# A wait in GpSimd's stream of gathers, moved behind the first gather of the next group

## The chip, the core and the metric

The kernel runs on one core of a Trainium2 chip. The metric is the device time of one execution in microseconds (us). The engines named here are TensorE (PE in the rows; its weight loads are PEld), VectorE (DVE), ScalarE (ACT), GpSimd (POOL) and SyncE (SP), which only issues transfers.

## The reference

For each of 512 samples, 26 embedding rows of 128 floats are looked up in 26 tables (1000 to 125000 rows each). The dense features are put in front as feature 0. The pairwise dot products of the 27 vectors are taken, and a three layer perceptron runs on the dense features and those products.

```python
e = jnp.stack([tbl_0[ids[:, 0]], ..., tbl_25[ids[:, 25]]], axis=1)      # 512 x 26 x 128
combined = jnp.concatenate([dense[:, None, :], e], axis=1)              # 512 x 27 x 128
interactions = jnp.einsum('bfd,bgd->bfg', combined, combined)
z = jnp.concatenate([dense, interactions[:, iu, ju]], axis=1)           # upper triangle, 351 pairs
h = jnp.concatenate([z, dense], axis=1)                                 # 512 x 607
h = jnp.maximum(h @ W_top1 + b_top1, 0.0)                               # 512
h = jnp.maximum(h @ W_top2 + b_top2, 0.0)                               # 256
y = h @ W_top3
```

## The kernel before

The 512 samples are four tiles of 128, t = 0 to 3. The rows of an embedding reach on-chip memory in one of two ways. Five features of every tile (six in the last two tiles) come from tables of 1000 rows that are loaded whole and multiplied by one-hot matrices on TensorE; the code calls such a step "hot". All other features are **gathered**: GpSimd issues one indirect transfer for each feature and tile, which fetches 128 rows of 512 bytes. Tiles 0 and 1 gather 21 features each, tiles 2 and 3 gather 20 each, 82 in all (line 419).

The gathers are put together in six groups for each tile, `g0` to `g5`, in the table `GROUPS`. Group 0 holds the dense features and three gathers, groups 1 to 4 hold four gathers (group 3 of tiles 2 and 3 holds three), group 5 holds two. Every group of every tile has a semaphore of its own, `rows_in[t][g]`, to which each of its gathers adds 16 when it has landed. TensorE waits on it ahead of the transposes of that group (line 681), and VectorE waits on groups 1 and 2 of tiles 2 and 3 ahead of dot products that it forms itself.

GpSimd walks through tiles, groups and gathers in that order. Ahead of a group's first gather it waits until all rows of the group before have landed (lines 414 to 417). From tile 2 on it also waits on `group_ps` ahead of the first gather of a tile, until TensorE has transposed the rows that stood in the same buffer two tiles earlier (`rows` has two slots, t % 2).

The order of the work on TensorE, ScalarE and VectorE is written out by hand in the table `ORDER`, one line for each tile. Its words are:

- `h`: eight chunks of one-hot products for one feature (lines 664, 667), stored by ScalarE at line 464
- `g0` to `g5`: the transposes of a group of the next tile (line 681), stored by ScalarE at line 485 or by VectorE at line 573. Products and transposes take turns in two banks of the product memory, so a step needs that the step two places before it is stored
- `u0`, `u1`: the pairwise products ("gram") of one half of this tile (line 702). ScalarE copies them to `z` (line 494), from tile 1 on together with VectorE (lines 586, 587)
- `x`, `l0` to `l3`, `e`, `y`: the perceptron (lines 647, 740, 752, 760 and 762), with its outputs taken out by ScalarE and VectorE
- `d`, `p`: dot products on VectorE and their transposition

So `u0` of a tile needs all six groups of that tile transposed and stored. For tiles 0 and 1 SyncE also moves parts of `z` by transfers once the copies are done, and the first layer waits for those.

```python
"h h g0 h g1 h g2 h g3-5",                       # ahead of tile 0
"u0 h u1 g0 h g1 h g2 h g3 h g4-5",              # tile 0, with the groups of tile 1 between
"u0-1 g0 h x0 l0:0 l1:0 g1 l2:0 l3:0 g2 e0 g3 d0-2:2 y0 x1 l0:1 l1:1 g4 d3-5:2 l2:1 g5 l3:1 e1",
"u0-1 y1 p2 d0-5:3 g0 x2 l0:2 g1 l1:2 g2 l2:2 g3 l3:2 e2 g4 y2 g5",
"u0-1 p3 x3 l0-3:3 e3 y3",
```

Of the kernel before, what the change touches and what calls it, by code (L numbers as in the profile page):

```python
# [27 lines left out]
def features(group):  # L28
    return [f + k for f, n in group for k in range(n)]
# [46 lines left out]
def dlrm_tower(nc, dense, ids, tables, w1, b1, w2, b2, w3, out):  # L76
# [20 lines left out]
    NG = len(GROUPS[0])  # L97
# [6 lines left out]
    gathered = [f for g in GROUPS[0] for f in features(g) if f]  # L104
# [43 lines left out]
    def fold_to(i):  # L148

        for k0, k1, src, _, to, at in folds():  # L150
            if k0 <= i // 4 < k1 and src // 32 == i % 4:
                return to + i // 4 - k0, at + 32 * (i % 4) + i + 1 - src


    assert all(m <= 4 * (to + k - k0) + at // 32 + 1 for k0, k1, _, m, to, at in folds() for k in range(k0, k1))
    PACKS = len(list(folds())) + 1

# [12 lines left out]
    def dot_at(i):  # L170

        first, _, _, at = PARTS[i >= PARTS[1][0]]
        return at + sum(NDOT - k for k in range(first, i))
# [26 lines left out]
    def groups_of(t):  # L200
        return GROUPS[t // HT]
# [4 lines left out]
    with ExitStack() as ctx:  # L206
        def sb(name, shape, dt=F32):
            return ctx.enter_context(nc.sbuf_tensor(name, shape, dt))

        def sem(name):  # L210
            return ctx.enter_context(nc.semaphore(name))

        ids_i = sb("ids_i", [P, T, NF - 1], I32)
# [3 lines left out]
        rows = sb("rows", [P, 2, len(gathered), D])  # L217
# [41 lines left out]
        rows_in = [[sem(f"rows_in{t}_{g}") for g in range(NG)] for t in range(T)]  # L259
# [140 lines left out]
        @block.gpsimd  # L400
        def _(pool):
            nc.gpsimd.memset(ident[:], 0.0).then_inc(ident_zeroed, 1)
            nc.gpsimd.iota(row_i[:], pattern=[[1, R8]], base=0, channel_multiplier=R8).then_inc(row_i_ready, 1)
            pool.wait_ge(ident_zeroed, 1)
            nc.gpsimd.affine_select(out=ident[:], in_=ident[:], compare_op=ALU.not_equal, fill=1.0, base=0,
                                    pattern=[[-1, P]], channel_multiplier=1).then_inc(ident_ready, 1)
            pool.wait_ge(ids_in, 16)
            for t in range(T):
                if t >= 2:

                    pool.wait_ge(group_ps, (t - 1) * NG)
                for g, group in enumerate(groups_of(t)):
                    if g:
                        pool.wait_ge(rows_in[t][g - 1], 16 * sum(f > 0 for f in features(groups_of(t)[g - 1])))
                    elif t:
                        pool.wait_ge(rows_in[t - 1][NG - 1], 16 * len(features(groups_of(t - 1)[NG - 1])))
                    for f in features(group):
                        if f:
                            pool.indirect_dma_start(  # L419
                                out=rows[:, t % 2, gathered.index(f), :], out_offset=None, in_=tables[f - 1],  # L420
                                in_offset=bass.IndirectOffsetOnAxis(ids_i[:, t, f - 1:f], 0),
                            ).then_inc(rows_in[t][g], 16)

        @block.scalar
        def _(act):
# [358 lines left out]
```

## Time and profile before

| what | value |
|---|---|
| median of 3 runs | 176.2 us (175.25 to 177.08) |
| the profiled execution's own time | 175.72 us |
| its span in the trace | 173.9 us |
| TensorE matmul busy | 118.4 us (68%) |
| TensorE weight load busy | 105.9 us (61%) |
| GpSimd busy | 79.8 us (46%), of it 79.0 us in 82 gathers |
| VectorE busy | 74.9 us (43%) |
| ScalarE busy | 72.3 us (42%) |
| mean granted TensorE clock | 0.80 of full speed |

The span runs from the first to the last recorded instruction; the execution's own time is 1.8 us longer. Busy shares are averages over stages with different limits. "issue" in a row is idle time of an engine for which the trace names no event. A gather's busy time is the time that GpSimd works on its descriptors; the rows land later.

### The profile page before, as it was taken

The numbers are of one execution on the slowest core, as the hardware profiler recorded it, in microseconds if no ns is written. First come the engines' busy times: TensorE is split into PE (matmuls) and PEld (weight loads), VectorE is DVE, ScalarE is ACT, GpSimd is POOL, SyncE is SP. The second block draws the span as 40 slices with busy tenths as digits, with TensorE's granted clock in tenths as the row PEclk, the third lists the DMA queues.
The fourth block names the chain that finished last, engine by engine and source line by source line (L and its number), as shares of the span: only waits on it lengthen the run. The fifth ranks groups of instructions, "written<-read, shape, count | busy, mean of one in ns | idle before, by whom it ended". The sixth has DMA issues, their size and how long they took to land.

```text
span 173.9 us, 2764 instructions
## 1 busy us (share of the span) xinstructions
PE 118.4 (68%) x1052; PEld 105.9 (61%) x1052; DVE 74.9 (43%) x181; ACT 72.3 (42%) x179; POOL 79.8 (46%) x89
## 2 busy tenths in 40 slices
PE   0699693621289729952886983849846499578694
PEld 0388583511189719841775983849735499467694
DVE  3699962960002545760062319900023994008200
ACT  7787873110109894421062831112023724208411
POOL 2662642644547547554645754546457455400000
PEclk9999879555557995795589999696987659969889
DMA  5645982573111111211111111211111112100000
GB/s 178 174 149 148 268 242 77 163 267 79 31 49 34 45 45 35 53 46 30 30 36 45 47 38 39 56 30 30 34 45 45 30 38 57 32 2 4 0 0 0
DMA packets 6290, 11.96 MB, mean 69 GB/s; under 512 B 2682, under 2 KB 3294, under 8 KB 6149
## 3 DMA queue, kind: packets, MB, share of 16 engines
q0 software_dynamic: 2624, 5.38, 12.1%
q1 hardware_dynamic: 3509, 6.15, 11.5%
q10 hardware_dynamic: 144, 0.26, 0.6%
q8 instruction: 8, 0.13, 0.3%
q14 instruction: 5, 0.04, 0.1%
HBM read 10.65 MB, written 0.00 MB: 61 GB/s over the span
## 4 chain that ended last, share of the span: by engine, by line
DMA 39%; POOL 32%; issue 15%; PE 8%; DVE 3%; POOLq 1%; ACT 0%
DMA rows<-in_tbl_dram,ids_i 37%; POOL rows L419 32%; PE ps L740 4%; DVE z L586 2%; PE ps L702 2%; DMA ids_i<-in_ids_dram 2%; PE ps L752 1%; PE ps L681 1%; POOLq L206 1%; PE ps L647 0%; DVE z L587 0%; PE ps L762 0%; ACT emb_t L485 0%; ACT y L521 0%; DVE h_t L614 0%
## 5 line engine op out<-in xcount | busy, mean ns | idle before, releaser
L419 POOL DMA_INDIRECT rows<-in_tbl_dram,ids_i x82 | 79.0, 964 | 70.1 <-DMA rows<-in_tbl_dram,ids_i 44.9
L552 DVE TENSOR_SCALAR hot<-ps,row_no 125x256 fp32r<-125x256 f32 x73 | 29.9, 474 | 26.0 <-PE ps L634 24.3
L681 PE MATMUL ps<-ident,rows 128*128 128x128 f32 x82 | 17.0, 333 | 30.8 <-DMA rows<-in_tbl_dram,ids_i 27.3
L494 ACT COPY z<-ps 32x80 f32<-32x80 f32 (+2 forms) x80 | 25.7, 321 | 28.3 <-remote 14.2
L681 PEld LDWEIGHTS ps<-ident,rows 128*128 128x128 f32 x82 | 11.0, 167 | 34.4 <-DMA rows<-in_tbl_dram,ids_i 30.0
L664 PE MATMUL ps<-hot,tab_hi 125*128 125x256 f32 x88 | 29.7, 357 | 2.8 <-ACT emb_t L464 1.5
L667 PE MATMUL ps<-hot,tab_lo 125*128 125x256 f32 x88 | 28.6, 345 | 1.2 <-DVE tab_lo L540 0.9
L702 PE MATMUL ps<-emb_t 128*64 128x52 f32 x512 | 23.9, 262 | 6.5 <-issue 3.7
L702 PEld LDWEIGHTS ps<-emb_t 128*64 128x64 f32 x512 | 22.0, 178 | 9.0 <-issue 6.3
L586 DVE COPY z<-ps 32x80 f32<-32x80 f32 (+2 forms) x42 | 13.1, 312 | 31.6 <-PE ps L702 18.6
L485 ACT COPY emb_t<-ps 128x512 f32<-128x512 f32 (+2 forms) x22 | 12.8, 580 | 32.5 <-PE ps L681 31.8
L664 PEld LDWEIGHTS ps<-hot,tab_hi 125*128 125x128 f32 x88 | 22.2, 253 | 3.9 <-ACT emb_t L464 1.7
L667 PEld LDWEIGHTS ps<-hot,tab_lo 125*128 125x128 f32 x88 | 22.1, 251 | 2.2 <-DVE tab_lo L540 1.2
L740 PE MATMUL ps<-z,w_pair 128*128 128x128 f32 x80 | 13.5, 334 | 2.1 <-DVE z L587 2.1
L740 PEld LDWEIGHTS ps<-z,w_pair 128*128 128x128 f32 x80 | 13.2, 250 | 2.6 <-ACT z L494 2.5
L614 DVE TENSOR_SCALAR h_t<-ps,b 128x128 f32<-128x128 f32 x4 | 1.4, 351 | 28.5 <-PE ps L752 28.5
L647 PE MATMUL ps<-emb_t,w_x 128*128 128x128 f32 x32 | 9.3, 403 | 4.4 <-issue 4.0
L509 ACT ACTIVATE h_t<-ps 128x128 f32<-128x128 f32 x16 | 4.4, 280 | 18.4 <-PE ps L740 12.1
L464 ACT COPY emb_t<-ps 128x256 f32<-128x256 f32 x11 | 6.6, 597 | 11.6 <-PE ps L667 8.7
L740 PEld LDWEIGHTS ps<-z,w_fold 128*128 128x128 f32 x64 | 9.8, 228 | 0.1
L740 PE MATMUL ps<-z,w_fold 128*128 128x128 f32 x64 | 9.7, 309 | 0.0
L752 PE MATMUL ps<-h_t,w 128*128 128x128 f32 x64 | 9.6, 311 | 0.0
(48 smaller groups left out, 96.4 us busy)
## 6 DMA issues: line engine op xcount, KB each, us to landing
tab<-in_tbl_dram SPq DMA_DIRECT2D x6, 448.0 KB
rows<-in_tbl_dram,ids_i POOLq DMA_INDIRECT x82, 2.6
w_fold<-w_pair SPq DMA_DIRECT2D x1, 1024.0 KB
w<-in_W_top_dram SPq DMA_DIRECT2D x1, 512.0 KB
tab<-in_tbl_dram SPq DMA_DIRECT2D x6, 52.0 KB
x_rows<-in_r_dense_features_dram ACTq DMA_DIRECT2D x1, 256.0 KB, 2.9
w_x<-in_W_top_dram SPq DMA_DIRECT2D x1, 256.0 KB
h_t<-in_W_top_dram SPq DMA_DIRECT2D x1, 256.0 KB
```

The source lines that it names most:

```text
L419: pool.indirect_dma_start(out=rows[:, t % 2, gathered.index(f), :], out_offset=None, in_=tables[f - 1], in_offset=bass.IndirectOffsetOnAxi ...
L485: nc.scalar.copy(*copies[-1]).then_inc(stored_act, 1)
L494: last = nc.scalar.copy(dst, src)
L552: nc.vector.tensor_scalar(hot[0:RP, k % OHB], ps[0:RP, IDV[h] + n % 2, 0:HB], row_no[0:RP, c:c + 1], None, ALU.is_equal).then_inc(hot_dve, 1)
L586: nc.vector.tensor_copy(dst, src)
L647: nc.tensor.matmul(block_ps(c), w_x[:, c * P:(c + 1) * P], emb_t[:, t, :, 0], start=True, stop=False)
L664: nc.tensor.matmul(bank, tab_hi[0:RP, n, c], one_hot, start=c == 0, stop=False)
L667: nc.tensor.matmul(bank, tab_lo[0:RP, n, c], one_hot, start=False, stop=c == R8 - 1).then_inc(hot_used, 1)
L681: last = nc.tensor.transpose(ps[:, ROT + bank_of(s), m * P:(m + 1) * P], src, ident[:])
L702: last = nc.tensor.matmul(ps[32 * q:32 * (q + GT), bank, col:col + GC], emb_t[:, t, b0:b0 + GT, :].rearrange("p b f -> p (b f)"), emb_t[:, ...
L740: last = nc.tensor.matmul(block_ps(c), weights[:, k, cols], z[:, t % 2, k, :], start=False, stop=k == nk - 1)
L752: last = nc.tensor.matmul(h2_ps(m), w_2[:, c, m * P:(m + 1) * P], h1_t[:, t % 2, c], start=c == 0, stop=c == NB - 1)
```

## The change

The wait for the group before is moved by one place: it stands behind the first gather of the new group and ahead of its second. The number of gathers, their order, their semaphores and all other engines' programs stay the same. The wait on `group_ps` at the start of tiles 2 and 3 stays ahead of the first gather.

```diff
                 for g, group in enumerate(groups_of(t)):
-                    if g:
-                        pool.wait_ge(rows_in[t][g - 1], 16 * sum(f > 0 for f in features(groups_of(t)[g - 1])))
-                    elif t:
-                        pool.wait_ge(rows_in[t - 1][NG - 1], 16 * len(features(groups_of(t - 1)[NG - 1])))
-                    for f in features(group):
-                        if f:
-                            pool.indirect_dma_start(
-                                out=rows[:, t % 2, gathered.index(f), :], out_offset=None, in_=tables[f - 1],
-                                in_offset=bass.IndirectOffsetOnAxis(ids_i[:, t, f - 1:f], 0),
-                            ).then_inc(rows_in[t][g], 16)
+                    fetched = [f for f in features(group) if f]
+                    for n, f in enumerate(fetched):
+                        if n == 1 and g:
+                            pool.wait_ge(rows_in[t][g - 1], 16 * sum(a > 0 for a in features(groups_of(t)[g - 1])))
+                        elif n == 1 and t:
+                            pool.wait_ge(rows_in[t - 1][NG - 1], 16 * len(features(groups_of(t - 1)[NG - 1])))
+                        pool.indirect_dma_start(
+                            out=rows[:, t % 2, gathered.index(f), :], out_offset=None, in_=tables[f - 1],
+                            in_offset=bass.IndirectOffsetOnAxis(ids_i[:, t, f - 1:f], 0),
+                        ).then_inc(rows_in[t][g], 16)
```

On GpSimd, at the start of tile 0 (the name behind `in_` is the table of a gather; `rows_in0_0` is group 0 of tile 0), the rows of both kernels differ like this:

```order
 L419 DMA rows<-in_tbl_1_dram,ids_i 128x128
 L419 DMA rows<-in_tbl_2_dram,ids_i 128x128
-L419 DMA rows<-in_tbl_18_dram,ids_i 128x128 [waits rows_in0_0]
-L419 DMA rows<-in_tbl_19_dram,ids_i 128x128
+L419 DMA rows<-in_tbl_18_dram,ids_i 128x128
+L419 DMA rows<-in_tbl_19_dram,ids_i 128x128 [waits rows_in0_0]
 L419 DMA rows<-in_tbl_20_dram,ids_i 128x128
 L419 DMA rows<-in_tbl_21_dram,ids_i 128x128
```

The gather from table 18, the first of group 1, no longer waits for group 0; the one behind it does. The same holds at every other border between two groups, 23 in all.

On GpSimd, around the start of tile 2, where a second semaphore is waited for:

```order
-L419 DMA rows<-in_tbl_7_dram,ids_i 128x128 [waits rows_in1_4]
-L419 DMA rows<-in_tbl_8_dram,ids_i 128x128
-L419 DMA rows<-in_tbl_0_dram,ids_i 128x128 [waits rows_in1_5,group_ps]
-L419 DMA rows<-in_tbl_1_dram,ids_i 128x128
+L419 DMA rows<-in_tbl_7_dram,ids_i 128x128
+L419 DMA rows<-in_tbl_8_dram,ids_i 128x128 [waits rows_in1_4]
+L419 DMA rows<-in_tbl_0_dram,ids_i 128x128 [waits group_ps]
+L419 DMA rows<-in_tbl_1_dram,ids_i 128x128 [waits rows_in1_5]
 L419 DMA rows<-in_tbl_2_dram,ids_i 128x128
```

The two waits that stood in front of one gather now stand in front of two different ones. In group 5, which has two gathers, the wait stands ahead of the last.

## Rows read from the trace of the kernel before

**Rows 1.** The chain of work that ended last, by engine, shares of the span.
```profile
DMA 39%; POOL 32%; issue 15%; PE 8%; DVE 3%; POOLq 1%; ACT 0%
```

**Rows 2.** Timeline, GpSimd, a quiet stretch: start, us, engine, line, [idle before <-releaser].
```profile
123.42 0.94 POOL L419 DMA_INDIRECT rows<-in_tbl_dram,ids_i  x1 [1.84 <-DMA rows<-in_tbl_dram,ids_i]
124.67 0.94 POOL L419 DMA_INDIRECT rows<-in_tbl_dram,ids_i  x1 [0.30 <-issue]
125.92 0.94 POOL L419 DMA_INDIRECT rows<-in_tbl_dram,ids_i  x1 [0.30 <-issue]
127.17 0.94 POOL L419 DMA_INDIRECT rows<-in_tbl_dram,ids_i  x1 [0.30 <-issue]
129.91 0.94 POOL L419 DMA_INDIRECT rows<-in_tbl_dram,ids_i  x1 [1.80 <-DMA rows<-in_tbl_dram,ids_i]
```

**Rows 3.** Waits of GpSimd, whole span: us in total, times, longest us.
```profile
POOL rows L419 <- DMA rows<-in_tbl_dram,ids_i: 44.9, 21, 5.4
```

**Rows 4.** Chain in order of time: from the last gather's start to its landing.
```profile
23.09 6.08 DMA rows<-in_tbl_dram,ids_i
...
33.18 3.10 DMA rows<-in_tbl_dram,ids_i
...
149.59 2.72 DMA rows<-in_tbl_dram,ids_i
```

**Rows 5.** Timeline, GpSimd, first gather of tile 2.
```profile
83.18 0.94 POOL L419 DMA_INDIRECT rows<-in_tbl_dram,ids_i  x1 [2.41 <-PE ps L681]
```

**Rows 6.** Timeline, TensorE: group transposes (L681) and gram (L702) of four tiles.
```profile
42.91 1.11 PE L681 MATMUL ps<-ident,rows 128*128 128x128 f32 x4 [5.47 <-DMA rows<-in_tbl_dram,ids_i]
...
48.63 3.66 PE L702 MATMUL ps<-emb_t 128*64 128x52 f32 x64 [1.04 <-ACT emb_t L485]
...
82.46 0.69 PE L681 MATMUL ps<-ident,rows 128*128 128x128 f32 x2 [2.98 <-DMA rows<-in_tbl_dram,ids_i]
83.91 6.31 PE L702 MATMUL ps<-emb_t 128*64 128x52 f32 x128 [0.77 <-ACT emb_t L485]
...
106.61 0.55 PE L681 MATMUL ps<-ident,rows 128*128 128x128 f32 x3 [2.87 <-DMA rows<-in_tbl_dram,ids_i]
...
113.38 0.65 PE L681 MATMUL ps<-ident,rows 128*128 128x128 f32 x4 [0.88 <-DMA rows<-in_tbl_dram,ids_i]
...
117.44 0.44 PE L681 MATMUL ps<-ident,rows 128*128 128x128 f32 x2 [2.07 <-DMA rows<-in_tbl_dram,ids_i]
...
122.54 2.58 PE L702 MATMUL ps<-emb_t 128*64 128x52 f32 x73
...
152.35 0.44 PE L681 MATMUL ps<-ident,rows 128*128 128x128 f32 x2 [2.27 <-DMA rows<-in_tbl_dram,ids_i]
153.66 5.27 PE L702 MATMUL ps<-emb_t 128*64 128x52 f32 x128 [0.88 <-ACT emb_t L485]
```

**Rows 7.** Waits of TensorE from 60 us to the end.
```profile
PE ps L681 <- DMA rows<-in_tbl_dram,ids_i: 13.2, 6, 3.0
```

**Rows 8.** Timeline, ScalarE: stores (L464, L485) and gram copies (L494).
```profile
77.76 0.59 ACT L464 COPY emb_t<-ps 128x256 f32<-128x256 f32 x1 [2.93 <-remote]
79.51 0.59 ACT L485 COPY emb_t<-ps 128x512 f32<-128x512 f32 x1 [1.16 <-PE ps L681]
...
87.91 2.81 ACT L494 COPY z<-ps 32x112 f32<-32x112 f32 x8 [4.36 <-PE ps L702]
...
129.24 2.42 ACT L494 COPY z<-ps 32x80 f32<-32x80 f32 x8 [7.92 <-remote]
```

**Rows 9.** Windows: stretch, length, busy us and (count) of PE, PEld, DVE, ACT, POOL, clock.
```profile
78.10:88.40 10.30, 6.26 (x87) 5.39 (x87) 0.47 (x2) 1.69 (x5) 4.72 (x5) 0.50 0.13 32
...
108.80:112.20 3.40, 3.40 (x18) 3.39 (x16) 3.16 (x8) 0.28 (x1) 2.36 (x3) 0.51 0.18 46
...
119.10:122.50 3.40, 3.40 (x17) 3.22 (x16) 0.00 (x0) 0.65 (x2) 1.89 (x2) 0.50 0.22 54
```

**Rows 10.** DMA queue of instructions: packets, MB, share of 16 engines.
```profile
q8 instruction: 8, 0.13, 0.3%
```

## Prediction

> **What bounds the kernel now.** I read the chain of work that ended last first. Transfers, GpSimd and its issue gaps fill 86% of it, TensorE 8% [rows 1]. The kernel is one long stream of gathers, with 20 us of other work behind the last. GpSimd's timeline shows the pattern. Four gathers start 1.25 us apart (0.94 busy and 0.30 to issue); then GpSimd sits idle 1.80 us, until the fourth has landed, and the next group's first gather starts 2.74 us behind it [rows 2]. There are 21 such waits, 44.9 us in total [rows 3], and two more at the starts of tiles 2 and 3, which the trace books to TensorE [rows 5]. The third view is TensorE's: what it waits for ahead of each tile's gram decides how much of a faster stream reaches the end. It stands idle 5.47 us ahead of one group of tile 0 and a few us more in later tiles [rows 6].
>
> **What one border costs, before and after.** Take the last gather of a group at time 0. Before, the next group's first gather starts at 2.74 and its second 1.25 later, at 3.99 [rows 2]. Now the first starts at 1.25 and is done at 2.19, while the landing that is waited for comes at about 2.5 in any case. The second then starts where the first stood, at 2.74. So each border gives 1.25 us, as long as the gather in flight doesn't hold up the landing. With 23 borders the stream of gathers gets 28.7 us shorter. At the starts of tiles 2 and 3 the two waits on one gather cost 2.41 us of idle time against 1.80 to 1.84 elsewhere [rows 2, 5]; split over two gathers, that 0.6 goes too, most likely (0.5 each taken, bounds 0 and 0.6). The last landing moves from 149.59 + 2.72 = 152.3 [rows 4] to about 152.3 - 28.7 - 1.0 = 122.6 us. TensorE can't follow that far, so the sum has to be made tile by tile at TensorE, at the start of each gram.
>
> **Tile 0.** The gram of tile 0 starts at 48.63, right behind the last two groups, for which TensorE waited [rows 6]. Five borders lie ahead of it: 5 x 1.25 = 6.2 us. TensorE's own work ahead of these groups ends long before (the idle 5.47 us of group 4 alone is nearly that). For the first three of these borders the row above doesn't hold, since table and weight loads are still moving and a landing takes 6.08 and 3.10 us there [rows 4]. If the gather that goes out early only queues in a line that is full already, those borders give nothing, and the gain is 2.5 us. If the idle line between groups is what is filled, they give more than 1.25 each, since each first gather then waits its long landing beside the previous one; I cap this at 8.7 us in all (2.5 us more). I take 6.2, as the borders with short landings give it and the idle line between groups is there in both cases.
> The trace shows that gathers land late only where the loads run [rows 4]. The Trainium skill, DMA: Bandwidth & Descriptors, section "Queues, rings and completion order", says that a DMA engine takes turns between the queues that have work for it, one packet at a time. By that, gathers beside loads go at the pace of their share, an earlier gather only waits earlier, and the three borders give near to nothing; the sum below would come to 160.1. The rows that are there before the change can't tell the two apart.
>
> **Tile 1.** Between tile 0's gram and the store at 77.76 [rows 8] no gather is waited for, so this piece moves as a whole. Then TensorE waited for groups 4 and 5, and the gram started at 83.91 [rows 6]. Without these waits, group 4 is transposed at once and its store (0.59) follows the one that ends at 78.35; group 5 needs the bank that this store frees, 0.69 for its two transposes, some 0.4 for its store and 0.4 to start: about 79.9. That gives 4.0 us (bounds 3.0, if the stores line up worse, and 5.1, the two idle times together). The rows are there: group 5's landing was at about 82.4 and ten to eleven borders have taken 12.5 to 13.7 us off it, against the 6.2 by which TensorE has moved.
>
> **Tile 2.** TensorE waited 2.87, 0.88 and 2.07 us for groups 3, 4 and 5 [rows 6], 5.8 us. Each landing is 18 us and more earlier by then, with TensorE 10 us earlier. What is late next is the first layer's wait for the moved parts of `z`, and stores on ScalarE, both nearly due at the same time. I take 5.5 (bounds 4.0 and 5.8).
>
> **Tile 3.** The last group's wait of 2.27 us [rows 6] goes. ScalarE's store of the group before and its copy of an output stand right behind it: 2.1 (bounds 1.5 and 2.3). The six waits of the last three tiles are 13.2 us by the view of waits [rows 7]; 11.6 of them count. From 153.66 on nothing of the tail (20.2 us) touches a gather, so it stays.
>
> **TensorE's clock.** The gram of tile 1, after idle time, ran with half the clock granted (1.2 in place of 2.4 GHz): its first half took from 83.91 to 87.91, 4.0 us [rows 6, 8, 9]. Two more stretches at half clock follow gather waits; in the three TensorE was busy 6.26 + 3.40 + 3.40 = 13.1 us [rows 9]. With the waits gone some of them may be granted in full, which halves their busy time: between nothing and 6.5 us. I take 2.0, the half of the one piece, those 4.0 us, on which both copying engines wait. The clock may as well fall at other places, which the rows of before can't show; I let that cost up to 1.5.
>
> **What stays.** VectorE and ScalarE started to copy the gram of tile 2 at 129.24 [rows 8], 6.7 us after it had begun at 122.54 with 73 matmuls in 2.58 us [rows 6]. There TensorE has gaps for which the trace names no event. I count them as unchanged. The page lists 8 instruction transfers of 0.13 MB together [rows 10]. The Trainium skill, Runtime: NRT & Kernel Launch, section "Instruction fetch mechanics", says that each engine's program is streamed in blocks of 16 KiB while it runs, at a cost that is mostly hidden. By that rule such gaps wouldn't be there; the trace doesn't agree if these gaps are fetches, which no row proves.
>
> **The sum.** 173.9 - 6.2 - 4.0 - 5.5 - 2.1 - 2.0 = 154.1 us of span. The execution's own time was 1.8 above its span, and the median of the runs 0.5 above that execution: 156.4 us.
>
> **Rivals.**
> - *Early borders give nothing and the clock stays.* For it: landings of 6.08 us [rows 4]. 156.4 + 3.7 + 2.0 = 162.1. Chance 0.17.
> - *More comes free.* The clock is granted in full at more places, tile 0 gains up to 8.7, or the gaps of tile 2 (6.7 us less the 2.58, 4.1) close as work shifts. For it: the low clock follows the waits for gathers [rows 6, 9]. About 156.4 - 2.5 - 2.5 = 151.4. Chance 0.18.
> - *The landing moves with the extra gather.* If a group counts as landed only when what is behind it in the queue is through, each landing comes later by what the border had given. Against it: within a group the gathers already follow at 1.25 us with the same number in flight, and the fourth lands 2.5 us after its start. At no gain per border the time is 176.2; at half of it tile 0 gains 3.1 and the later waits mostly still go, about 160 to 168. Chance 0.08.
> - *Slower.* The place is the same landing, with the point of decision at 1.25 us: if an extra gather in flight puts the landing back by more than that, every border loses. Were it by 1.5 us, 23 x 0.25 = 5.8 us would be lost on the path, 182 us. It could be so if GpSimd's descriptor work on the new gather held up the completion of the old one. Against it: that work is 0.94 us and over 0.3 us before the landing is due. Chance 0.02.
> - *The change doesn't do what it says.* GpSimd's order shows each wait moved by one gather at all borders; only if GpSimd stopped for the index list or a hidden limit of gathers in flight would the time stay at 176. Chance 0.02.
>
> **How the numbers follow.** The forecast as written, 153 to 160, has 0.53. With the rivals on either side, 151 to 164 holds about 8 in 10: it reaches 151.4 and 162.1 and a part of the third rival. A change of 1% (1.8 us) is about what a measurement of this kernel can tell from none. Faster by over 1%: 0.94, within 1%: 0.03, slower: 0.03.
>
> **What would show it.** In the profile after, GpSimd's idle time ahead of a group's second gather is about 0.55 us (2.74 - 1.25 - 0.94), its last gather starts near 120 us, and the chain of waits no longer runs through gathers behind tile 0. TensorE waits for rows in tile 0 alone, its grams start near 42.4, 73.7, 105 to 107 and 133 to 136 us, and the tail of 20 us is as long as before. I am wrong if the landing after a group's last gather is well over 2.6 us in the quiet part, if the gram of tile 0 starts later than 44, or if new idle time on ScalarE's or SyncE's side takes over in tile 2.

## The result and the profile after

The changed kernel took 147.63 us (147.18 to 148.24, four runs) against 175.85 us (175.25 to 177.08, four runs) for the kernel before: a ratio of 0.839, 95% interval 0.8333 to 0.8447. The forecast was 156.4 us with a range of 151 to 164, so the sign was right and the gain, 28.2 us, was larger than the range allowed. The experiments below add a second finding that matters more for anyone who wants to use the change: measured again on three other chips, the same changed kernel took 208 to 210 us, while the kernel before took 176 everywhere. First the execution that the forecast was about.

The page: the first row of busy times, and the chain of work that ended last.

```profile
PE 103.3 (71%) x1052; PEld 93.8 (65%) x1052; DVE 75.0 (52%) x181; ACT 72.3 (50%) x179; POOL 80.0 (55%) x89
...
DMA 46%; POOL 27%; issue 13%; PE 9%; DVE 3%; ACT 1%; POOLq 0%
```

Against [rows 1], nothing has taken the place of the gathers: transfers, GpSimd and issue gaps are still 86% of the chain, and the span is 145.4 us in place of 173.9. The waits of GpSimd and of TensorE, whole span (us in total, times, longest):

```profile
POOL rows L419 <- DMA rows<-in_tbl_dram,ids_i: 21.0, 22, 3.6
...
PE ps L681 <- DMA rows<-in_tbl_dram,ids_i: 17.7, 9, 4.2
```

GpSimd's waits fell from 44.9 us [rows 3] to 21.0. TensorE, though, still waits nine times for gathers, seven of them behind 60 us, which the forecast had said it would not do behind tile 0. GpSimd's timeline after, a quiet stretch and the last gather:

```profile
97.38 0.94 POOL L419 DMA_INDIRECT rows<-in_tbl_dram,ids_i  x1 [0.48 <-DMA rows<-in_tbl_dram,ids_i]
98.63 0.94 POOL L419 DMA_INDIRECT rows<-in_tbl_dram,ids_i  x1 [0.31 <-issue]
...
101.47 0.94 POOL L419 DMA_INDIRECT rows<-in_tbl_dram,ids_i  x1 [0.65 <-DMA rows<-in_tbl_dram,ids_i]
...
121.37 0.94 POOL L419 DMA_INDIRECT rows<-in_tbl_dram,ids_i  x1 [0.56 <-DMA rows<-in_tbl_dram,ids_i]
```

Where 1.80 us of idle time stood at a border [rows 2], 0.48 to 0.65 stand now. The last gather starts at 121.37; before it was 149.59 [rows 4]. TensorE's timeline after, with the group transposes (L681) that waited and the grams (L702):

```profile
36.82 1.11 PE L681 MATMUL ps<-ident,rows 128*128 128x128 f32 x4 [4.22 <-DMA rows<-in_tbl_dram,ids_i]
41.08 0.69 PE L681 MATMUL ps<-ident,rows 128*128 128x128 f32 x2 [3.14 <-DMA rows<-in_tbl_dram,ids_i]
42.64 3.59 PE L702 MATMUL ps<-emb_t 128*64 128x52 f32 x64 [0.87 <-ACT emb_t L485]
...
70.61 0.44 PE L681 MATMUL ps<-ident,rows 128*128 128x128 f32 x2 [1.89 <-DMA rows<-in_tbl_dram,ids_i]
71.81 3.94 PE L702 MATMUL ps<-emb_t 128*64 128x52 f32 x128 [0.77 <-ACT emb_t L485]
...
97.17 0.44 PE L681 MATMUL ps<-ident,rows 128*128 128x128 f32 x2 [0.69 <-DMA rows<-in_tbl_dram,ids_i]
100.65 3.94 PE L702 MATMUL ps<-emb_t 128*64 128x52 f32 x128
...
123.94 0.44 PE L681 MATMUL ps<-ident,rows 128*128 128x128 f32 x2 [1.69 <-DMA rows<-in_tbl_dram,ids_i]
125.25 5.15 PE L702 MATMUL ps<-emb_t 128*64 128x52 f32 x128 [0.88 <-ACT emb_t L485]
```

Set beside [rows 6], the pieces between the starts of the grams are:

| piece of the span | before | after | gain | forecast |
|---|---|---|---|---|
| to the gram of tile 0 | 48.63 | 42.64 | 6.0 | 6.2 |
| from there to the gram of tile 1 | 35.28 | 29.17 | 6.1 | 4.0 |
| to the gram of tile 2 | 38.63 | 28.84 | 9.8 | 5.5, and most of the clock's 2.0 |
| to the gram of tile 3 | 31.12 | 24.60 | 6.5 | 2.1 |
| tail | 20.2 | 20.15 | 0.1 | 0 |

Two details of the table: the gram of tile 1 took 6.31 us at half clock before [rows 6] and 3.94 now, and the gram of tile 2, which had gaps before, is one dense block of 128 matmuls. ScalarE's row for that gram after is

```profile
102.77 4.89 ACT L494 COPY z<-ps 32x80 f32<-32x80 f32 x16 [2.54 <-PE ps L702]
```

2.1 us behind the gram's start, where it had been 6.7.

### The profile page after: what moved, and what is told of

It is laid out like the page before. It is cut to its first block, busy times and chain, and to the rows that moved or that the text cites. A ratio compares the mean times of both kernels' runs of the same rounds, so it can differ in the third digit from the quotient of the medians.

```text
span 145.4 us, 2762 instructions
## 1 busy us (share of the span) xinstructions
PE 103.3 (71%) x1052; PEld 93.8 (65%) x1052; DVE 75.0 (52%) x181; ACT 72.3 (50%) x179; POOL 80.0 (55%) x89
## 3 DMA queue, kind: packets, MB, share of 16 engines
q0 software_dynamic: 2624, 5.38, 14.0%
## 4 chain that ended last, share of the span: by engine, by line
DMA 46%; POOL 27%; issue 13%; PE 9%; DVE 3%; ACT 1%; POOLq 0%
DMA rows<-in_tbl_dram,ids_i 44%; POOL rows L419 27%; PE ps L740 4%; DVE z L586 3%; PE ps L702 2%; DMA ids_i<-in_ids_dram 2%; PE ps L752 1%; PE ps L647 1%; DVE z L587 0%; PE ps L762 0%; PE ps L681 0%; ACT emb_t L485 0%; ACT y L521 0%; DVE h_t L614 0%; POOLq L206 0%
## 5 line engine op out<-in xcount | busy, mean ns | idle before, releaser
L494 ACT COPY z<-ps 32x80 f32<-32x80 f32 (+2 forms) x80 | 25.8, 323 | 13.8 <-PE ps L702 12.9
L664 PE MATMUL ps<-hot,tab_hi 125*128 125x256 f32 x88 | 27.7, 340 | 4.4 <-ACT emb_t L464 4.3
L681 PE MATMUL ps<-ident,rows 128*128 128x128 f32 x82 | 15.1, 304 | 21.2 <-DMA rows<-in_tbl_dram,ids_i 17.7
L667 PE MATMUL ps<-hot,tab_lo 125*128 125x256 f32 x88 | 26.7, 329 | 1.7 <-DVE tab_lo L540 1.7
L681 PEld LDWEIGHTS ps<-ident,rows 128*128 128x128 f32 x82 | 9.8, 152 | 24.3 <-DMA rows<-in_tbl_dram,ids_i 19.7
L485 ACT COPY emb_t<-ps 128x512 f32<-128x512 f32 (+2 forms) x22 | 12.7, 579 | 24.7 <-PE ps L681 24.5
L664 PEld LDWEIGHTS ps<-hot,tab_hi 125*128 125x128 f32 x88 | 20.7, 235 | 5.4 <-ACT emb_t L464 4.8
L667 PEld LDWEIGHTS ps<-hot,tab_lo 125*128 125x128 f32 x88 | 20.8, 236 | 2.2 <-DVE tab_lo L540 2.2
L702 PE MATMUL ps<-emb_t 128*64 128x52 f32 x512 | 18.7, 241 | 2.5 <-ACT emb_t L485 2.5
L702 PEld LDWEIGHTS ps<-emb_t 128*64 128x64 f32 x512 | 18.1, 157 | 3.6 <-ACT emb_t L485 2.1
L740 PE MATMUL ps<-z,w_pair 128*128 128x128 f32 x80 | 11.7, 302 | 2.2 <-DVE z L587 2.2
L740 PEld LDWEIGHTS ps<-z,w_pair 128*128 128x128 f32 x80 | 11.4, 218 | 2.6 <-ACT z L494 2.5
L601 DVE TENSOR_TENSOR prod<-rows 128x384 f32<-128x384 f32 (+2 forms) x18 | 8.5, 473 | 4.6 <-issue 4.0
L464 ACT COPY emb_t<-ps 128x256 f32<-128x256 f32 x11 | 6.6, 604 | 7.8 <-PE ps L667 7.7
```

The costliest lines, as they stand in the source:

```text
L485: nc.scalar.copy(*copies[-1]).then_inc(stored_act, 1)
L494: last = nc.scalar.copy(dst, src)
L601: nc.vector.tensor_tensor(prod[:, 0:n], left.to_broadcast([P, n, D]), rows[:, t % 2, right:right + n, :], ALU.mult).then_inc(prod_ready, 1)
L664: nc.tensor.matmul(bank, tab_hi[0:RP, n, c], one_hot, start=c == 0, stop=False)
L667: nc.tensor.matmul(bank, tab_lo[0:RP, n, c], one_hot, start=False, stop=c == R8 - 1).then_inc(hot_used, 1)
L681: last = nc.tensor.transpose(ps[:, ROT + bank_of(s), m * P:(m + 1) * P], src, ident[:])
```

## The experiments

Two questions stood. Why did TensorE follow the stream all the way? And, from chip B on, why does the changed order make the kernel slower there? The runs fell on five chips, called A (the first four), B (the next four), C, D and E, one set of runs on each and in this order of time; the kernel before ran beside each set and took 176.74, 176.43, 176.25, 176.42 and 176.03 us in the median. A ratio is to the kernel before of the same set.

### Chip A: what bounds the kernel

**The kernel before, unchanged.**

> The kernel before, unchanged, profiled once more. Theory A (TensorE's gaps in the first profile of before, at 92 to 94 and 125 to 129 us, belong to its code and the changed kernel removes them): they come again at the same places, and ScalarE's copies of tile 2's gram start some 6.7 us after the gram. Theory B (the gaps are an accident of one execution and cost nothing there, because a later wait for gathers swallows them): they are gone or stand elsewhere, while the span stays at 174 us within 1. Under both the time is 176 us.

It took 175.65 us, span 173.8. Its timelines of TensorE and ScalarE:

```profile
84.64 6.61 PE L702 MATMUL ps<-emb_t 128*64 128x52 f32 x128 [0.77 <-ACT emb_t L485]
...
122.93 3.94 PE L702 MATMUL ps<-emb_t 128*64 128x52 f32 x128
...
125.05 5.00 ACT L494 COPY z<-ps 32x80 f32<-32x80 f32 x16 [2.54 <-PE ps L702]
```

The gaps in tile 2's gram are gone, and the span is the same to 0.1 us. So they had cost nothing: the waits for gathers behind them had swallowed them. "I count them as unchanged" kept about 4 us in the forecast that were not work. The same two executions show how large this slack is. TensorE's waits for gathers from 60 us on:

```profile
PE ps L681 <- DMA rows<-in_tbl_dram,ids_i: 23.3, 9, 3.7
```

In the first trace of the same kernel they were 13.2 us in six waits [rows 7]. TensorE was busy for 118.4 us there and for 112.2 here, and the span is the same. So some 10 us that one trace shows as TensorE's own work and gaps are waits for gathers in the other. The forecast took off only what the first trace named.

**No gathers at all.** The 82 gathers and their waits are left out, `rows` is filled with a constant, and TensorE and VectorE wait for that filling alone:

```diff
-            for t in range(T): ...   # all gathers and their waits
+            nc.gpsimd.memset(rows[:, 0], 0.25).then_inc(rows_in[0][0], 1)
+            nc.gpsimd.memset(rows[:, 1], 0.25).then_inc(rows_in[1][0], 1)
```

> All 82 gathers are left out, so the output is not the reference's: GpSimd fills the two row buffers with a constant once, and TensorE and VectorE wait for that alone. What remains is the time of all other work. Theory A, the prediction's step that TensorE and its partners can't follow the faster stream (their own work taken from the trace of before with its gaps and low clock): 148 to 156 us, so that in the changed kernel little of the gathers was left on the path. Theory B (the stream of gathers sets the changed kernel's time all along and the rest is much shorter than I took it for): 120 to 140 us.

124.34 us (124.09 to 126.69), ratio 0.7034 (0.6957 to 0.7112), span 122.2. The chain by engine:

```profile
PE 54%; ACT 16%; DVE 15%; issue 7%; DMA 5%; SPq 0%; ACTq 0%; DVEq 0%
```

This is the floor of all work other than gathers. The changed kernel's 145.4 is 23 us above it, so there was room to follow the stream everywhere, also behind tile 0.

**The wait one gather further back.**

```diff
-                        if n == 1 and g:
+                        if n == min(2, len(fetched) - 1) and g:
-                        elif n == 1 and t:
+                        elif n == min(2, len(fetched) - 1) and t:
```

> The wait stands behind the second gather of the new group in place of the first (in the groups of two gathers it stays ahead of the second). Stream theory: in the changed kernel each border still has some 0.55 us of idle time on GpSimd ahead of the second gather, 0.3 of it beyond the ordinary issue gap; now the landing is over before the third gather is due, so about 0.25 us for each of 23 borders and a bit more in the first 36 us: 6 to 9 us under the changed kernel, 139 to 142 us. Rival (the rest of the work binds by now): 145 to 148 us. Rival (more gathers in flight hold up each other's landing): slower than the changed kernel, over 149 us.

141.05 us (140.54 to 142.13), ratio 0.7998 (0.7917 to 0.8079), span 138.8.

**No wait between groups.**

```diff
-                        if n == 1 and g:
-                            pool.wait_ge(rows_in[t][g - 1], ...)
-                        elif n == 1 and t:
-                            pool.wait_ge(rows_in[t - 1][NG - 1], ...)
```

> No wait between groups at all (the wait for the row buffer at the start of tiles 2 and 3 stays). Stream theory: 82 gathers every 1.25 us end near 107 us, with the landing 109 us; then the rest of the work sets the time, somewhere between the time without any gathers and 142 us. Rival (a limit on transfers in flight, for which the waits were put in): gathers get longer than 0.94 us or the loads of tables are held up in the first 36 us, and it is no faster than with the wait behind the first gather, 147 us or more.

133.78 us (133.49 to 134.13), ratio 0.7568 (0.7502 to 0.7633), span 132.0. The chains of the last two runs, and the last gather of the second:

```profile
POOL 45%; DMA 24%; issue 16%; PE 9%; DVE 3%; ACT 1%; POOLq 0%
```

```profile
POOL 59%; issue 20%; PE 10%; DMA 4%; DVE 4%; POOLq 1%; ACT 1%
...
107.73 0.94 POOL L415 DMA_INDIRECT rows<-in_tbl_dram,ids_i  x1 [0.30 <-issue]
```

From the start of the last gather to the end of the span it is 24.3 us in the kernel before (173.9 - 149.59), 24.0 in the changed one (145.4 - 121.37), 23.0 with the wait behind the second gather (138.8 - 115.77) and 24.3 without waits (132.0 - 107.73). While the last gather's start moves by 42 us, the way from it to the end changes by 1.3 us at most. That settles the first question for these executions: the end follows the last gather.

### Chip B: the gain in parts

The new order was used at some borders alone and the old one at the rest, by the number of gathers ahead of the wait (0 or 1):

```diff
-                        if n == 1 and g:
+                        if n == (CONDITION) and g:
-                        elif n == 1 and t:
+                        elif n == (CONDITION) and t:
```

CONDITION is `t == 0`, then `t == 0 and g <= 3`, then `t == 1`, then `t >= 2`.

> The wait stands behind the first gather only within tile 0 (5 of 23 borders). Tile by tile theory of the prediction: the gram of tile 0 starts 6.2 us earlier, and since later waits for gathers then are again what TensorE waits for, the end moves by about 6.2 us: 170 us. Stream theory: the same, 5 x 1.25 = 6.2 and perhaps a little more for the late landings. Both expect 169 to 171; only the term itself is tested.

171.24 us (170.51 to 171.93), ratio 0.9677 (0.9611 to 0.9744): 5.7 us (4.5 to 6.9) of the 6.2.

> Only the first three borders are changed (groups 1 to 3 of tile 0), where loads still move and landings take 4 to 6 us. If a gather only queues in a line that is full there, they give under 1 us together: 175 to 176.5. If the gap between groups was idle line, they give 3.7 us or more: 173 or less.

174.74 us (173.25 to 174.95), ratio 0.9861 (0.9789 to 0.9933). By the ratio that is 2.5 us (1.2 to 3.7) for the three early borders, against 3.7 at 1.25 each and 0 if a gather only queued. The rest of tile 0's gain, 5.7 - 2.5 = 3.2 us, is that of the two quiet borders, where 2.5 was forecast. The early ones do give something. That each gives less than a quiet one is what the medians say; the interval reaches up to the full 3.7.

> Only the six borders into and within tile 1 are changed. Prediction's sum by tiles: 4.0 us, the end of TensorE's waits in that tile as the other work allows (172 us). Stream theory (a late tile waits for gathers in any case, so every border counts in full at the end): 6 x 1.25 = 7.5 us, 169 us.

179.27 us in the median of ten runs that lay from 172.74 to 183.15: no gain that can be told, where 4.0 or 7.5 us were expected, and the widest spread so far.

> Only the twelve borders into and within tiles 2 and 3 are changed. Prediction's sum by tiles: 5.5 + 2.1 = 7.6 us and perhaps 2 from the clock, 166 to 169 us. Stream theory: 12 x 1.25 = 15.0 us and 1.2 for the two places with two waits, as far as TensorE follows: 160 to 162 us.

201.4 us (200.89 to 202.3), ratio 1.1407 (1.1333 to 1.1482). The stream of gathers had become shorter as planned: its last gather starts at 134.05, 15.5 us earlier than before. But the end came at 199.4. TensorE's waits and its timeline say where:

```profile
PE ps L702 <- issue: 40.8, 38, 2.6
...
84.70 3.59 PE L702 MATMUL ps<-emb_t 128*64 128x52 f32 x56 [0.77 <-ACT emb_t L485]
88.55 0.25 PE L702 MATMUL ps<-emb_t 128*64 128x52 f32 x1 [0.26 <-issue]
89.26 0.33 PE L702 MATMUL ps<-emb_t 128*64 128x52 f32 x4 [0.47 <-issue]
...
131.69 0.24 PE L702 MATMUL ps<-emb_t 128*64 128x52 f32 x1 [2.45 <-issue]
...
138.75 0.99 PE L702 MATMUL ps<-emb_t 128*64 128x52 f32 x14 [0.45 <-issue]
```

The gram of tile 1 starts as usual with 56 matmuls in 3.59 us. Then TensorE issues one or a few instructions and stands idle for 0.3 to 2.6 us, over and over, for 50 us, and no semaphore is named that it would wait for. It runs freely again at 138.75, 4.7 us behind the start of the last gather. The rows at 88.55 and 89.26 are 0.71 us apart; the other steps are that or about two, three or four times that. I call this the **slow issue**. It makes the second question, and the forecast had no rival for it. The other grams of this execution are the best comparison there is, on the same chip and in the same 200 us: of the 40.8 us of idle time, 39.7 fall in the gram of tile 1, beside which gathers go out in the new order. The gram of tile 0, beside gathers with the old rests, has 1.1 us, and those of tiles 2 and 3, with no gather beside them, have none (128 matmuls in 3.94 us each).

### Chip C: is it the kernel or the chip?

The same two kernels again, the changed kernel unchanged, and the new order in tiles 0 and 1 (`t <= 1`).

> The kernel with only the twelve borders of tiles 2 and 3 changed, a second time. In the first run its gathers ended at 134 us as the stream theory has it, but TensorE issued the matmuls of tile 1's gram at steps of 0.7 us and multiples of it for 51 us. If that is a property of this program, it comes again: 200 to 203 us, with the same gaps in the same gram. If it is a state of a chip or of one loading of the program, it is gone and the time is 160 to 163 us.

201.68 us (200.79 to 202.5), ratio 1.1444 (1.1381 to 1.1507). TensorE's wait for issue at line 702 is 40.8 us again, 39.6 of it in tile 1's gram.

> The kernel with only the six borders of tile 1 changed, a second time. A property of the program: 173 to 183 us again, with slow issue in tile 0's gram (49 to 81 us). A state of the chip: 168 to 170 us, 7.5 us under before.

178.7 us (178.28 to 180.92), ratio 1.0166 (1.0094 to 1.0239). The new order in tile 1 alone costs 3 us here (1.7 to 4.2). Of 18.6 us of slow issue 14.8 are in tile 0's gram, beside which tile 1's gathers run.

> The changed kernel itself, on this chip. 147 to 148 us and no gaps within a gram if the slow issue belongs to programs; if it belongs to the chip, it may now show it as well and be slower than 147.6.

209.93 us (207.56 to 211.46), ratio 1.1868 (1.1778 to 1.1958). The very kernel that gave 147.63. Its waits of TensorE and GpSimd, and its gram of tile 0:

```profile
PE ps L702 <- issue: 56.9, 52, 2.6
...
POOL rows L419 <- PE ps L681: 22.2, 1, 22.2
...
42.98 3.42 PE L702 MATMUL ps<-emb_t 128*64 128x52 f32 x52 [0.87 <-issue]
46.64 0.31 PE L702 MATMUL ps<-emb_t 128*64 128x52 f32 x3 [0.23 <-issue]
...
70.16 0.24 PE L702 MATMUL ps<-emb_t 128*64 128x52 f32 x1 [1.85 <-issue]
...
98.20 1.97 PE L702 MATMUL ps<-emb_t 128*64 128x52 f32 x32 [1.17 <-issue]
...
119.09 0.34 PE L702 MATMUL ps<-emb_t 128*64 128x52 f32 x5 [0.38 <-issue]
```

The gram starts at 42.98, where it started in the first measurement (42.64): up to there the two executions are alike. The stream of gathers then runs on, since it doesn't need TensorE until tile 2, and has to stop there for 22.2 us, between a gather that starts at 93.21 and the next at 116.31. TensorE follows that stop: at 98.20, 5.0 us behind the gather of 93.21, it runs the last 32 matmuls of the gram in 1.97 us, and it works without such gaps until the gathers are back; at 119.09, 2.8 us behind the first of them, the steps begin again. 56.9 us of idle time in grams is most of the 60.2 us by which this span (205.6) is longer than 145.4.

> The eleven borders of tiles 0 and 1 are changed, tiles 2 and 3 keep the old order. Stream theory: 11 x 1.25 = 13.7 us, 162 to 163 us. Sum by tiles of the prediction: 6.2 + 4.0 = 10.2 us, 166 us. If slow issue strikes: more, with gaps in a gram.

171.2 us (169.94 to 173.46), ratio 0.9692 (0.9623 to 0.9761). The gain of tile 0 (5.7 on chip B) is all that is left. There are 21.3 us of slow issue, 15.9 of them in tile 0's gram, where tile 1's share is lost; the waits for later gathers absorb a part. The other 5.4 us are in the grams of tiles 1 and 2, beside gathers that keep the old rests.

### Chip D: what does it need?

The changed kernel as control, the kernel without gathers again, the changed kernel with plain transfers in place of the gathers, and the kernel without waits.

> The changed kernel a third time, as the control of this set. Its first measurement gave 147.6 us with no gaps inside a gram, the second, on another chip, 209.9 us with gaps at steps of 0.7 us for 52 us in tile 0's gram and 26 us in tile 1's. If a state of the chip decides, this one shows one of the two again (147 or 208), and the other kernels of this set take the same side.

208.35 us (207.46 to 209.38), ratio 1.1803 (1.1729 to 1.1876): this chip shows it too.

> All gathers are left out, so the output is not the reference's. If the control is slow: theory C (TensorE's slow issue needs the stream of gathers beside it) says 124 us and no gaps inside a gram; theory D (TensorE's supply of instructions is slow on that chip whatever GpSimd does, whenever many small matmuls follow each other) says gaps in every gram and 150 us or more. If the control is fast, both say 124.

124.07 us (123.57 to 126.41), ratio 0.702 (0.698 to 0.7059), the same as on chip A, with every gram dense. The grams alone don't do it.

```diff
-                        pool.indirect_dma_start(
-                            out=rows[:, t % 2, gathered.index(f), :], out_offset=None, in_=tables[f - 1],
-                            in_offset=bass.IndirectOffsetOnAxis(ids_i[:, t, f - 1:f], 0),
-                        ).then_inc(rows_in[t][g], 16)
+                        pool.dma_start(out=rows[:, t % 2, gathered.index(f), :],
+                                       in_=tables[f - 1][128 * t:128 * (t + 1), :]).then_inc(rows_in[t][g], 16)
```

This one fetches 128 neighbouring rows, not the rows of the indices.

> Each gather is replaced by a plain load of 128 neighbouring rows of the same table, issued by GpSimd in the same order with the same waits, so the output is not the reference's; the bytes and the row length stay. If the control is slow and the slow issue comes from the traffic of rows or from GpSimd issuing any transfer, it stays (over 190 us, or at least gaps in the grams). If it comes from the index reading or the single scattered rows of a gather, it goes. If the control is fast, this shows what a plain load costs GpSimd in the same place, 147 us or less.

131.43 us (130.59 to 132.06), ratio 0.7438 (0.7398 to 0.7478), and no gap in any gram. The group of these loads, with GpSimd's idle time ahead of them:

```profile
L419 POOL DMA_DIRECT2D rows<-in_tbl_dram x82 | 43.6, 539 | 52.0 <-DMA rows<-in_tbl_dram 49.0
```

The same bytes and packets (5.38 MB in 2624) by the same queue with the same waits don't disturb TensorE. But this run changes two things at once: a load keeps GpSimd busy for 539 ns in place of 966, and so GpSimd rests at the borders again (49.0 us of waits, as in the kernel before). It clears the bytes and the packets, not the density of GpSimd's own work.

> No wait between groups. It took 133.8 us on a chip without slow issue. If the control is slow, theory C says that TensorE crawls while the stream lasts: the gram of tile 0 starts near 42 and ends only when GpSimd stops for the row buffer at the start of tile 2 (near 60 us), then again in tile 1 or 2: between 150 and 210 us, with the crawl ending where GpSimd's stream ends.

216.16 us (213.02 to 218.44), ratio 1.2086 (1.2022 to 1.215), against 133.78 on chip A. With no rests at all the two outcomes lie further apart than with short ones. The expectation missed: the time is above its 210, and the gram of tile 0, due near 42, starts at 74.50. The delay stands ahead of the gram (all engines on one time axis):

```profile
57.08 0.95 POOL L415 DMA_INDIRECT rows<-in_tbl_dram,ids_i  x1 [0.30 <-issue]
64.37 0.59 ACT L460 COPY emb_t<-ps 128x256 f32<-128x256 f32 x1 [33.49 <-remote]
64.41 0.88 DVE L548 TENSOR_SCALAR hot<-ps,row_no 125x256 fp32r<-125x256 f32 x2 [22.38 <-remote]
65.02 0.58 PE L660 MATMUL ps<-hot,tab_hi 125*128 125x256 f32 x1 [24.91 <-ACT emb_t L460]
```

The gather of 57.08 is the last before GpSimd has to stop for the row buffer. ScalarE and VectorE had stood for 33.5 and 22.4 us, with nothing local named as the releaser, and both start 7.3 us behind that gather; TensorE had waited 24.9 us for ScalarE.

### Chip E: gathers kept away from the grams

```diff
                     fetched = [f for f in features(group) if f]
+                    if t and g == 1:
+                        pool.wait_ge(gram_ps, t * NU)
```

GpSimd waits ahead of the second group of tiles 1 to 3 until the gram of the tile before is through.

> The changed kernel with one wait more at each of the borders between the first and the second group of tiles 1 to 3: GpSimd waits there until TensorE has run the whole gram of the tile before. So no gather goes out beside the dense part of a gram, and the stream of gathers stands still some 8 us three times. If the slow issue of TensorE needs gathers that follow each other without a pause beside a gram (theory D), the grams are free of gaps whatever chip this lands on, each takes about 6.6 us, and the time is that of the changed kernel in the first measurement plus three holds, 147.6 + 3 x 8 = some 165 to 174 us. If what disturbs TensorE is the order of the gathers or the program's layout as such, and not their company at the gram (theory E), gaps of 0.7 us and more are in the grams here too where the control shows them, and the time is above 185.

> The changed kernel once more, unchanged, as control for the run beside it. On a chip with the slow issue it gives 205 to 212 us with gaps in the grams of tiles 0 and 1; on one without it 147 to 149. Both were seen; three of four measurements of kernels that gather without pauses beside the grams of tiles 0 and 1 came out slow, so 208 is the likelier.

The control took 208.31 us (207.51 to 211.41), ratio 1.1818 (1.1701 to 1.1935), with 55.7 us of slow issue. The kernel with the holds took 189.67 us (185.54 to 191.69). Its timelines: the grams of tiles 0 and 1 on TensorE and one hold on GpSimd, a stretch outside the grams, and GpSimd's waits for the grams.

```profile
45.35 3.66 PE L704 MATMUL ps<-emb_t 128*64 128x52 f32 x64 [0.87 <-ACT emb_t L487]
...
51.53 2.08 PE L704 MATMUL ps<-emb_t 128*64 128x52 f32 x64
...
90.87 3.94 PE L704 MATMUL ps<-emb_t 128*64 128x52 f32 x128 [0.77 <-ACT emb_t L487]
...
53.89 0.94 POOL L421 DMA_INDIRECT rows<-in_tbl_dram,ids_i  x1 [7.70 <-PE ps L704]
...
65.44 0.41 PE L669 MATMUL ps<-hot,tab_lo 125*128 125x256 f32 x1
65.78 0.58 PE L636 MATMUL ps<-ids_t,ident_r 26*128 26x256 f32 x1
...
72.67 0.59 ACT L466 COPY emb_t<-ps 128x256 f32<-128x256 f32 x1 [8.57 <-remote]
72.70 3.23 DVE L554 TENSOR_SCALAR hot<-ps,row_no 125x256 fp32r<-125x256 f32 x8 [7.35 <-remote]
...
POOL rows L421 <- PE ps L704: 41.1, 3, 19.5
```

The grams are dense, on a chip whose control has them full of gaps. So the slow issue inside a gram needs gathers beside it, as theory D said. But its time of 165 to 174 us was missed by 11 to 18 us, and by the time alone theory E (above 185) would have been right. The three holds took 41.1 us where 24 had been reckoned, since TensorE reached its grams late, and the four rows ahead of the last show one place where it lost time. ScalarE's store at 72.67 needs the products that TensorE finished at 65.85 (65.44 + 0.41), and VectorE's comparisons at 72.70 need the broadcast of 65.78, done at 66.36. Nothing local is named as the releaser, and both start within 0.03 us of each other, 6 to 7 us late, while gathers run at 1.25 us. So the disturbance reaches further than TensorE's instruction issue: ScalarE and VectorE start late too while the gathers run without long pauses. The control shows the same sign, and more of it (TensorE, GpSimd, VectorE and ScalarE on one time axis):

```profile
48.54 0.21 PE L702 MATMUL ps<-emb_t 128*64 128x52 f32 x1 [0.37 <-issue]
55.01 0.37 PE L634 MATMUL ps<-ids_t,ident_r 26*128 26x256 f32 x1 [0.42 <-issue]
...
61.82 0.94 POOL L419 DMA_INDIRECT rows<-in_tbl_dram,ids_i  x1 [0.54 <-DMA rows<-in_tbl_dram,ids_i]
...
63.53 5.46 ACT L494 COPY z<-ps 32x112 f32<-32x112 f32 x16 [20.57 <-remote]
...
93.16 3.22 DVE L552 TENSOR_SCALAR hot<-ps,row_no 125x256 fp32r<-125x256 f32 x8 [55.26 <-remote]
```

The first half of tile 0's gram is done at 48.75, and ScalarE copies it at 63.53, 15 us later. The broadcast of 55.01 is done at 55.38, and VectorE's comparisons on it start at 93.16, 38 us later. Meanwhile GpSimd's gathers run at their usual pace, and the border at 61.82 shows 0.54 us of idle time as in the first measurement. So GpSimd isn't slowed, and TensorE, ScalarE and VectorE are. "Slow issue" names only the part that TensorE shows. Theory D looked at that part alone, which is the likely reason why 165 to 174 us was too low; no run separates it.

## Why the prediction was right and wrong

**The border** was right. 23 borders at 1.25 us and two double waits were to bring the last landing from 152.3 to 122.6; it landed at 123.9, 28.4 us earlier. The idle time ahead of the second gather (0.55 forecast) is 0.48 to 0.65 in the quiet part.

**Tile 0** was right: 6.0 us measured, 6.2 forecast, and 5.7 with the new order there alone. The early borders give 2.5 of their 3.7 us (1.2 to 3.7). What the prediction drew from the Trainium skill's rule of turns between queues (DMA: Bandwidth & Descriptors, "Queues, rings and completion order"), that they would give near to nothing (sum 160.1), fell; the rule itself was not tested.

**"TensorE can't follow that far"** is the step that failed. It made the sum from pieces of TensorE's time in the old execution, with only the waits for gathers taken off, as if all else in a piece were work. It was not. In the pieces that end at the grams of tiles 1, 2 and 3 the forecast took off 11.6 us and 2.0 for the clock; they shrank by 22.4. The repeated run of the kernel before shows the size of the error: the waits for gathers behind 60 us, which the forecast read as 13.2 us, are 23.3 us in another execution of the same kernel with the same span. What the first trace had in place of these 10 us is seen in two places. The gaps in tile 2's gram (about 4 us) were absorbed, since the repeated run of the kernel before has none and the same span. And the half clock fell on dense matmuls that stood between waits: matmul busy time fell from 118.4 to 103.3 us, though the instructions are the same 1052, and the mean clock rose from 0.80 to 0.88. (6.2 of these 15.1 us also fell between the two executions of the kernel before, without any gain in span.) Looking back, a second method was at hand: the larger of the kernel without gathers (122.2 us of span, which only a run could tell) and the stream with its tail (122.6 + 21.6, the way from the last landing to the end, 173.9 - 152.3) is 144.2 us of span; it was 145.4. How the 8.8 us that these pieces gave beyond the forecast divide between gaps, clock and other slack isn't shown; that the piecewise sum was the wrong method is.

**"What stays"**: the Trainium skill's rule on instruction fetch (Runtime: NRT & Kernel Launch, "Instruction fetch mechanics") was weighed against gaps in a gram. Whether those gaps are fetches no run shows. They look like a mild form of the slow issue, with steps of 0.7 us or twice that. On chip B the kernel with the new order in tile 0 alone shows 5.0 us of them, and gained what was expected all the same.

**The clock** was sized at 2.0 with an upper end of 6.5 us of busy time. Busy time fell by 15.1, of which 6.2 lie within what two executions of the kernel before differ by. The term was too small, and it was no separate term: where TensorE waits for gathers afterwards anyway, a faster matmul only makes the wait longer.

**The rivals.** "More comes free" went the right way and stopped at 151.4, since it too was built on the pieces. "The landing moves" and "early borders give nothing" fell. "Slower" was given 0.03 in all, 0.02 of it to its one mechanism, a landing put back by the extra gather. In the measurement that the forecast was about it fell; on chips C, D and E the changed kernel was slower by 18 to 19%, by a mechanism that is not in the prediction at all, while the borders there are as short as ever (0.54 us at 61.82).

**What stays open.** The slow issue grows with the density of indirect gathers beside a gram. On chips B and C the profiled executions show at most 3.8 us of it in a gram beside gathers that keep the old rests of 1.8 us, and 12.8 to 39.7 us where the rests are 0.5 us; a gram with no gather beside it has none. It doesn't come from the gram alone, nor from the same bytes by plain loads. It wasn't there in every set of runs: the first measurement and chip A were free of it in the kernels with dense gathers, B to E had it. The kernel before is at 176 us in all of them. Since each chip was measured once, and the two free sets came first, these runs can't tell a property of a chip from one that came with time. The first profile of the kernel before has 3.7 us of these gaps, and the repeated one on chip A none; whether such gaps in a kernel give the warning beforehand was not tried. Why a set has it, and what resource GpSimd's gathers and the other engines share, was not found out. Late instruction fetches are one rival: the page lists the same 8 instruction transfers of 0.13 MB in the first measurement and on chips B to E, so not more is fetched, but when each block arrived isn't shown. Another is the recording of the executions (each timed run comes with a granted clock, so none ran unrecorded). A gather whose descriptors keep GpSimd busy for 0.5 us at the same density, or dense gathers beside an otherwise empty TensorE, were not tried.

## What to carry to other kernels

When a stream (here the gathers) is sped up, bound the result from two sides with whole runs or whole chains, the stream plus its tail and the kernel without the stream, and take the larger; the pieces between waits of an old execution hold slack that isn't named as waiting, and two executions of one kernel can name 13.2 and 23.3 us of it. That bound held here in executions without the slow issue, and was drawn up after the result. A rest in one engine's stream can be what keeps the others going: before such a change is kept, time it on several chips and more than once, since one median here is 16% faster and another 19% slower. Here the robust part is the new order in tile 0 alone, where no gram runs beside it, 3% faster on the chip where it was tried (0.9677), and on another, with tile 1 added, no worse (0.9692), though neither was run on chip A.

## What the runs showed of the hardware

- An indirect gather of 128 rows takes GpSimd 0.94 us and 0.30 to the next, lands about 2.5 us after its start in a quiet stretch, and all 82 behind each other without a wait kept that pace on chip A (81 gaps of 0.3 us, last start at 107.73).
- Beside such gathers, in four of six sets of runs (chips B to E), TensorE's small matmuls (128x64 weights, 52 columns) fell from some 30 ns each (128 in 3.94 us) to one or a few per 0.71 us or a multiple, for as long as the gathers went on: 39.7 and 39.6 us of idle time in one gram, and 55.7 to 56.9 in two. It ended about 5 us behind the start of the last gather ahead of a stop (98.20 after 93.21, 138.75 after 134.05), and began again 2.8 us behind the first one after it.
- On such a chip ScalarE and VectorE started work 6 to 7 us after what it needs was done, both at the same moment (72.67 and 72.70), and with the grams not held 15 and 38 us after it (63.53 and 93.16). Without any rest they stood for 33.5 and 22.4 us, until 7.3 us behind the last gather ahead of a stop. GpSimd's own gathers kept their pace.
- A plain load of the same 64 KB by GpSimd's queue costs GpSimd 539 ns, an indirect one 966.
